# The experts' bias as one fp32r product of the 0/1 choice, with the probability multiplied in afterwards

## Chip, cores and metric

The kernel runs on one core of a Trainium2 chip. The metric is the device time of one execution in microseconds (us); the median of several runs is given.

## What is computed

The input is x, 4 images of 64 x 64 x 64, and a class token. Three layers follow: an involution over the image, a layer norm with a state space model in both directions, and a layer norm with a mixture of experts. The change lies in the last one:

```python
H = jax.nn.gelu(xf @ W1 + b1, approximate=False)          # 256 hidden values per token
probs = jax.nn.softmax(H @ Wg + bg, axis=-1)              # 8 experts
assign = jnp.argmax(probs, axis=-1)
for e in range(8):
    y = H @ Wd[e] + bd[e]
    out = out + jnp.where((assign == e)[:, None], probs[:, e:e + 1] * y, 0.0)
```

Each token takes the one expert with the highest probability, and that expert's output, its bias bd included, is multiplied by the probability. The layer's input is added to it.

## The kernel before

The kernel is a row of blocks (setup, involution, matrices, layer norm, state space, experts), each with one hand-written instruction order per engine and semaphores between the engines. At a block's end all engines wait for one another.

The function experts works on 17 items: 16 of 512 columns, each holding 1024 tokens as 8 groups (TPI) of 128 tokens, and a last small one for the 4 class tokens. A loop over windows runs on every engine; window i holds the main work of item i and preparations of items i+1 to i+4.

- TensorE (PE), in the order of its function window (L1390): hide (L1320) makes the hidden values of item i+1 in two halves; speak (L1363) makes, for one group of 128 tokens, the outputs of all 8 experts, 6 fp32r products of 128x512 each (L1374); there are 8 speaks per window, t = 0 to 7. Between them stand turn_gate (L1357, the transposition of the gate), turn_out and turn_in (transpositions for later items), judge (L1333, the logits of item i+1, after speak 4), gates (L1348), and add_bias (L1380, after speak 6).
- add_bias multiplies the transposed gate, in which each token has the probability of its expert in one of 8 places and zeros elsewhere, by bd8, which holds bd eight times along a diagonal of blocks. This is one fp32 product of 64 rows and 512 columns (L1386); it shows as two instructions in the trace. It writes the PSUM tensor pGR, which judge uses too.
- VectorE (DVE), in the order of its function window (L1594): multiply (L1505) takes the 8 experts' outputs of a group from PSUM times the gate; part (L1517) makes the low part of a piece of the hidden values of item i+1 (four pieces, between the multiplies of tiles 0 to 3); minus_sum, low and normalise prepare later items; finish (L1585) adds the bias of item i-1, read from pGR, to the experts' sum and stands behind the multiply of tile 3; choose_best (L1544) and weigh_best (L1565) make the gate of item i+1 in 11 small steps around the multiply of tile 6.
- ScalarE (ACT) does the gelu, copies the transposed gate to SBUF (keep_gate, L1442), and works on squares and copies for later items.
- GpSimd (POOL) adds the 8 experts' products of four groups in a tree (L1669, L1671, L1673, L1678), twice per window: the first tree after the multiply of tile 3, the second after that of tile 7. Between the two stands the factor of item i+3 (L1650 to L1660), with a pow at L1652, which normalise waits for.
- SP stores the results; the loads of weights, bd among them, are issued early by SP in load_rest (L475), in the block of the involution.

A speak needs one of three PSUM buffers and waits for the multiply three tiles back. judge waits for the last part of its item. finish releases pGR: judge and add_bias wait on its semaphore, finished.

Before the first item, the windows -3 to 0 only prepare (AHEAD = 4).

Of the kernel before, what the change touches and what calls it, by code (L numbers as in the profile page):

```python
# [34 lines left out]
class Tower:  # L35


    def __init__(self, nc, ctx, arrays, out):
# [19 lines left out]
        self.bd8 = sb("bd8", [2 * TILES * EX, 2 * TILES, F])  # L58
# [413 lines left out]
FFN_LOADS = 17  # L472


def load_rest(sp, g, m):  # L475
# [15 lines left out]
    for t in range(2 * TILES):  # L491
        sp.dma_start(g.bd8[EX * t:EX * t + EX, t, :], g.bd).then_inc(m.ffn_in, 16)
# [711 lines left out]
def experts(nc, g):  # L1204
# [8 lines left out]
    with ExitStack() as ctx:  # L1213
# [15 lines left out]
        pT = pLT[0:TPI * EX, 4 * TILES * EX:]  # L1229
# [16 lines left out]
        gT = sb("gT", [TPI * EX, 128])  # L1246
        gl = sb("gl", [128, 5, TPI, EX])
        gate = [sb(f"gate{n}", [128, TPI, EX]) for n in range(2)]
# [6 lines left out]
        picked = [sb(f"picked{n}", [128, TPI, F]) for n in range(2)]  # L1255
        res = [sb(f"res{n}", [128, TPI, F]) for n in range(2)]
# [8 lines left out]
        gate_turned, gate_kept, biased = sem("gate_turned"), sem("gate_kept"), sem("biased")  # L1265
# [5 lines left out]

        hflat = g.hT[:].rearrange("p b r q -> p (b r q)")
# [25 lines left out]
        with nc.Block() as block:  # L1298
            @block.tensor
            def _(pe):  # L1300
# [32 lines left out]
                def judge(i):  # L1333
# [3 lines left out]
                    if i >= 2:  # L1337
                        pe.wait_ge(finished, i - 1)
# [18 lines left out]
                def turn_gate(i):  # L1357
                    pe.wait_ge(dv, GATE * (i + 1))
                    P, G = rows(i), groups(i) * EX
                    nc.tensor.transpose(pT[0:G, 0:P], gate[i % 2][0:P, 0:groups(i), :].rearrange("p t e -> p (t e)"),  # L1360
                                        g.ident[0:P, 0:P]).then_inc(gate_turned, 1)
# [67 lines left out]
            def _(act):  # L1429
# [12 lines left out]
                def keep_gate(i):  # L1442
# [3 lines left out]
                    P, G = rows(i), groups(i) * EX  # L1446
                    nc.scalar.copy(gT[0:G, 0:P], pT[0:G, 0:P]).then_inc(gate_kept, 1)
# [39 lines left out]
                for i in range(1 - AHEAD, ITEMS):  # L1487
# [12 lines left out]
                    if there(i + 4):  # L1500
                        rest(i + 4)

            @block.vector
            def _(v):
# [39 lines left out]
                def choose_best(i):  # L1544
# [18 lines left out]
                    nc.vector.tensor_tensor(G(1), G(1), wide(s(1)), ALU.is_equal).then_inc(dv, 1)  # L1563

                def weigh_best(i):  # L1565
# [12 lines left out]
                    nc.vector.reciprocal(s(3), s(2)).then_inc(dv, 1)  # L1578
                    v.wait_ge(dv, base + 10)
                    if i >= 2:  # L1580
                        v.wait_ge(gate_turned, i - 1)
                    nc.vector.tensor_tensor(gate[i % 2][0:P, 0:T, :], G(1), s(3).unsqueeze(2).broadcast_to([P, T, EX]),
                                            ALU.mult).then_inc(dv, 1)
# [53 lines left out]
                for i in range(1 - AHEAD, ITEMS):  # L1637
                    window(i)
                finish(NCH)
# [100 lines left out]
```

## Time and profile before

| | us |
|---|---|
| runs (3) | 689.91, 690.77, 691.05 |
| median | 690.77 |
| profiled execution, its own time | 688.56 |
| its span, first to last instruction | 686.5 |

| engine | busy us | share of the span |
|---|---|---|
| PE | 608.6 | 89% |
| DVE | 495.9 | 72% |
| POOL | 403.8 | 59% |
| ACT | 263.6 | 38% |

The profile is one execution of the kernel on the chip. Times are microseconds from the span's start unless marked ns. PE is TensorE's matmuls, PEld its loads of weights, which lie beside them. L1374 is line 1374 of the kernel. out<-in names the tensor written and those read, x16 counts instructions. A matmul's end is modelled and matmuls are pipelined, so two that follow one another overlap in the rows; from the start of one group to the start of the next is the better measure. On DVE, too, an instruction can start some 0.1 us before the one ahead of it is over in the rows.

### The profile page before, as it was taken

How to read it: one execution, taken by the hardware profiler on the slowest of the kernel's cores; microseconds unless marked ns; L12 is line 12 of the kernel's file. 1: busy time of each engine (PE TensorE's matmuls, PEld its weight loads, DVE VectorE, ACT ScalarE, POOL GpSimd, SP SyncE). 2: the span in 40 equal slices, each digit the busy share in tenths (PEclk: the TensorE clock that was granted, in tenths of full speed). 3: DMA queues.
4: the chain of work that ended last, by engine and by line, in shares of the span. 5: the costliest groups of instructions: out<-in, count | busy, mean ns of one | idle time of the engine just before them, and what ended most of it. 6: DMA issues, size and time to landing. Idle time of an engine off the chain costs nothing. (4 is left out here: it accounts for less than half of the span.)

```text
span 686.5 us, 9721 instructions
## 1 busy us (share of the span) xinstructions
PE 608.6 (89%) x3015; PEld 435.9 (64%) x3015; DVE 495.9 (72%) x948; ACT 263.6 (38%) x689; POOL 403.8 (59%) x562
## 2 busy tenths in 40 slices
PE   0799899967967899999973899999999999999995
PEld 0477777754745787878752466666666666666662
DVE  6688888873895787888832567777777777777664
ACT  2132223224651222222225555555555555545310
POOL 1689999610351133333345167778777777778756
PEclk9999999997977999999985599999999999999998
DMA  6200000000000000000000000000000000000001
GB/s 249 48 1 0 0 1 1 0 0 1 0 0 1 0 1 1 0 0 0 1 0 0 1 1 16 16 17 16 17 16 16 16 16 15 3 16 17 15 17 31
DMA packets 13011, 9.75 MB, mean 14 GB/s; under 512 B 4396, under 2 KB 12716, under 8 KB 12716
## 3 DMA queue, kind: packets, MB, share of 16 engines
q1 hardware_dynamic: 12956, 9.28, 4.4%
q8 instruction: 19, 0.31, 0.2%
q14 instruction: 20, 0.16, 0.1%
q10 hardware_dynamic: 16, 0.00, 0.0%
HBM read 5.08 MB, written 4.20 MB: 14 GB/s over the span
## 5 line engine op out<-in xcount | busy, mean ns | idle before, releaser
L1374 PE MATMUL ex_pE<-ex_WdP,ex_hid 128*128 128x512 f32 x774 | 205.9, 408 | 0.0
L1374 PEld LDWEIGHTS ex_pE<-ex_WdP,ex_hid 128*128 128x128 f32 x774 | 140.0, 189 | 44.3 <-DVE ex_ms L1514 7.7
L1514 DVE TENSOR_TENSOR ex_ms<-ex_pE,ex_gate 128x512 f32<-128x512 f32 x129 | 88.9, 689 | 73.3 <-PE ex_pE L1374 71.4
L1669 POOL TENSOR_TENSOR ex_s<-ex_ms 128x1024 f32<-128x1024 f32 (+1 forms) x33 | 82.4, 2497 | 66.0 <-DVE ex_ms L1514 66.0
L723 DVE TENSOR_TENSOR inv_prod<-inv_pW,m_img 128x504 f32<-128x504 f32 x144 | 91.7, 681 | 17.4 <-PE inv_pW L638 15.7
L1195 POOL TENSOR_TENSOR hT<-hT,ssm_gelu 128x512 f32<-128x512 f32 x32 | 47.7, 1509 | 95.8 <-ACT ssm_gelu L1168 95.8
L649 PE MATMUL inv_pS<-ident,inv_prod 128*128 128x128 f32 x576 | 87.8, 275 | 6.1 <-DVE inv_prod L723 5.4
L649 PEld LDWEIGHTS inv_pS<-ident,inv_prod 128*128 128x128 f32 x576 | 70.0, 141 | 28.6 <-DVE inv_prod L723 20.7
L638 PE MATMUL inv_pW<-inv_ysb,m_conv2L 98*128 98x512 f32 x144 | 69.4, 485 | 2.3 <-DVE inv_ysb L711 2.3
L1438 ACT ACTIVATE ex_hidf<-ex_pH,b1c 128x512 f32<-128x512 f32 (+1 forms) x68 | 45.1, 664 | 60.8 <-PE ex_pH L1327 60.8
L1065 PE MATMUL ssm_y<-ssm_z,N 128*128 128x512 f32 x192 | 52.1, 408 | 6.7 <-DVE ssm_z L1130 6.5
L1151 ACT CAST ssm_z<-ssm_back 128x512 fp32r<-128x512 f32 x32 | 18.3, 618 | 102.4 <-DVE ssm_back L1127 102.4
L1520 DVE TENSOR_TENSOR ex_hid<-ex_hidf,ex_hid 128x512 fp32r<-128x512 f32 (+1 forms) x68 | 55.8, 841 | 1.2 <-ACT ex_hid L1438 1.2
L1032 PE MATMUL ssm_v<-u,LV 128*128 128x512 f32 (+1 forms) x192 | 50.1, 407 | 0.0
L1130 DVE TENSOR_TENSOR ssm_z<-ssm_back,ssm_z 128x512 fp32r<-128x512 f32 x32 | 36.1, 1169 | 19.3 <-ACT ssm_z L1151 19.3
L1671 POOL TENSOR_TENSOR ex_s<-ex_s 128x512 f32<-128x512 f32 (+1 forms) x33 | 46.5, 1409 | 2.6
L1065 PEld LDWEIGHTS ssm_y<-ssm_z,N 128*128 128x128 f32 x192 | 36.8, 194 | 17.5 <-DVE ssm_z L1130 8.9
L1438 ACT ACTIVATE ex_hid<-ex_pH,b1c 128x512 fp32r<-128x512 f32 (+1 forms) x68 | 45.2, 665 | 0.0
L1461 ACT ACTIVATE ex_sq<-ex_hs,ex_stat 128x64 f32<-128x64 f32 (+1 forms) x130 | 43.6, 351 | 0.8 <-DVE ex_stat L1528 0.8
L688 ACT COPY hT<-inv_pS 128x256 f32 (+1 forms) x32 | 10.5, 382 | 81.8 <-PE inv_pS L649 81.8
L1032 PEld LDWEIGHTS ssm_v<-u,LV 128*128 128x128 f32 x192 | 36.1, 192 | 8.1
L800 POOL TENSOR_TENSOR u<-ln_u,u 128x512 fp32r<-128x512 f32 x14 | 18.6, 1352 | 37.9 <-ACT u L869 37.9
(238 smaller groups left out, 1022.9 us busy)
## 6 DMA issues: line engine op xcount, KB each, us to landing
m_img<-in_x SPq DMA_DIRECT2D x2, 2048.0 KB, 9.2
out<-ex_res SPq DMA_DIRECT2D x16, 256.0 KB, 2.3
WdT<-in_L_ffn_Wd SPq DMA_DIRECT2D x2, 256.0 KB
W1d<-in_L_ffn_W SPq DMA_DIRECT2D x2, 64.0 KB
bd<-in_L_ffn_bd SPq DMA_DIRECT2D x8, 2.0 KB
m_Bm<-in_L_attn_fwd_B_real SPq DMA_DIRECT2D x2, 16.0 KB, 1.9
m_Bm<-in_L_attn_fwd_B_imag SPq DMA_DIRECT2D x2, 16.0 KB, 2.0
m_Bm<-in_L_attn_bwd_B_real SPq DMA_DIRECT2D x2, 16.0 KB, 2.0
```

Source lines behind the costliest of these rows:

```text
L638: nc.tensor.matmul(pW[k % NW][:], m.conv2L[:, k, :], ysb[u][:], start=True, stop=True).then_inc(weighed, 1)
L649: last = nc.tensor.matmul(pS[:, 128 * j:128 * j + 128], prod[:, k, 2 * j:2 * j + 2, :], g.ident[:], is_transpose=True, start=(k == 0 and j ...
L723: nc.vector.tensor_tensor(prod[:, k, :, lo:hi], pW[k % NW][:, :, lo:hi], rows[:, :, lo + dw:hi + dw], ALU.mult).then_inc(filtered, 1)
L1032: last = nc.tensor.matmul(out[:], g.LV[weight][:, LVI[d][t][q], :], cols(g.u[value], b, d, h, q), start=(q == 0 and (value, weight) == PAR ...
L1065: last = nc.tensor.matmul(out, g.N[weight][:, n, d, first:first + 2, :], before(zP[n][value], d, h), start=False, stop=(n == 1 and (value, ...
L1195: nc.gpsimd.tensor_tensor(t, t, act_y[n % 4][:], ALU.add).then_inc(summed, 1)
L1374: last = nc.tensor.matmul(pE[n % 3][0:P].rearrange("p e f -> p (e f)"), hid[i % 2][value][:, h, par, 128 * j:128 * j + P], WdP[weight][:, ...
L1438: last = nc.scalar.activation(o[:, h, par, 0:cols(i)], pH[par][:, 0:cols(i)], ACT.Gelu, bias=g.b1c[:, h:h + 1])
L1514: nc.vector.tensor_tensor(ms[b % NB][0:P, t % TPB, :].rearrange("p (e f) -> p e f", e=EX), pE[n % 3][0:P], gate[i % 2][0:P, t, :].unsqueez ...
L1520: nc.vector.tensor_tensor(hid[i % 2][1][:, h, par, c], hidf[:, h, par, c], hid[i % 2][0][:, h, par, c], ALU.subtract).then_inc(parted, 1)
L1669: nc.gpsimd.tensor_tensor(s4[0:P, 0:T], m[:, :, 0:4 * F], m[:, :, 4 * F:], ALU.add).then_inc(halved, 1)
L1671: nc.gpsimd.tensor_tensor(s2[0:P, 0:T], s4[0:P, 0:T, 0:2 * F], s4[0:P, 0:T, 2 * F:], ALU.add).then_inc(quartered, 1)
```

## The change

The transposed tensor is no longer the gate but the 0/1 choice, `hot`, written twice side by side (64 and 64 columns, so 128 rows after the transposition). Zeros and ones are exact in fp32r. The right side becomes `bdP`, in fp32r: its upper 64 rows hold bd rounded to fp32r, its lower 64 rows the remainder, so that one fp32r product of 128 rows gives the bias of the chosen expert. VectorE then multiplies it by the probability, kept in `best`, in a new step keep_bias, which moves it from PSUM to the SBUF tensor `bias`; finish adds `bias` and `picked`, both in SBUF. bd is loaded 16 times for 8. ScalarE and VectorE make bdP once, in the first preparing window. judge and add_bias wait for bias_kept in place of finished. turn_gate waits for step 6 of the item's 11 instead of the last.

```diff
-FFN_LOADS = 17
+FFN_LOADS = 25
...
-    for t in range(2 * TILES):
-        sp.dma_start(g.bd8[EX * t:EX * t + EX, t, :], g.bd).then_inc(m.ffn_in, 16)
+    for t in range(4 * TILES):
+        sp.dma_start(g.bd8[EX * t:EX * t + EX, t % (2 * TILES), :], g.bd).then_inc(m.ffn_in, 16)
...
                     if i >= 2:
-                        pe.wait_ge(finished, i - 1)
+                        pe.wait_ge(bias_kept, i - 1)
...
                 def turn_gate(i):
-                    pe.wait_ge(dv, GATE * (i + 1))
-                    P, G = rows(i), groups(i) * EX
-                    nc.tensor.transpose(pT[0:G, 0:P], gate[i % 2][0:P, 0:groups(i), :].rearrange("p t e -> p (t e)"),
+                    pe.wait_ge(dv, GATE * i + 6)
+                    P = rows(i)
+                    nc.tensor.transpose(pT[:, 0:P], hot[i % 2][0:P].rearrange("p v t e -> p (v t e)"),
                                         g.ident[0:P, 0:P]).then_inc(gate_turned, 1)
...
                     if i >= 1:
-                        pe.wait_ge(finished, i)
-                    P, G = rows(i), groups(i)
-                    nc.tensor.matmul(pGR[0:P, 0:F * G], gT[0:EX * G, 0:P],
-                                     g.bd8[0:EX * G, 0:G, :].rearrange("k t f -> k (t f)"),
-                                     start=True, stop=True).then_inc(biased, 1)
+                        pe.wait_ge(bias_kept, i)
+                    else:
+                        pe.wait_ge(bd_parted, 1)
+                    P = rows(i)
+                    nc.tensor.matmul(pGR[0:P], gT[:, 0:P], bdP[:], start=True, stop=True).then_inc(biased, 1)
...
-                    nc.scalar.copy(gT[0:G, 0:P], pT[0:G, 0:P]).then_inc(gate_kept, 1)
+                    P = rows(i)
+                    nc.scalar.copy(gT[:, 0:P], pT[:, 0:P]).then_inc(gate_kept, 1)
...
+                    if i == 1 - AHEAD:
+                        nc.scalar.copy(bdh[lower], bd[lower])
+                        nc.scalar.copy(bdP[upper], bd[upper]).then_inc(bd_high, 1)
...
-                    nc.vector.tensor_tensor(G(1), G(1), wide(s(1)), ALU.is_equal).then_inc(dv, 1)
+                    if i >= 2:
+                        v.wait_ge(gate_turned, i - 1)
+                    both = lambda a: a.unsqueeze(1).broadcast_to([P, 2, T, EX])
+                    nc.vector.tensor_tensor(hot[i % 2][0:P, :, 0:T, :], both(G(1)),
+                                            s(1).unsqueeze(1).unsqueeze(3).broadcast_to([P, 2, T, EX]), ALU.is_equal).then_inc(dv, 1)
...
+                def keep_bias(i):
+                    v.wait_ge(biased, i + 1)
+                    P, T = rows(i), groups(i)
+                    nc.vector.tensor_tensor(bias[i % 2][0:P, 0:T, :], pGR[0:P, 0:F * T].rearrange("p (t f) -> p t f", f=F),
+                                            best[i % 2][0:P, 0:T].unsqueeze(2).broadcast_to([P, T, F]), ALU.mult).then_inc(bias_kept, 1)
...
-                    v.wait_ge(biased, i + 1)
+                    v.wait_ge(bias_kept, i + 1)
...
-                    nc.vector.tensor_tensor(res[i % 2][0:P, 0:T, :].rearrange("p t f -> p (t f)"), pGR[0:P, 0:F * T],
-                                            picked[i % 2][0:P, 0:T, :].rearrange("p t f -> p (t f)"), ALU.add).then_inc(finished, 1)
+                    nc.vector.tensor_tensor(res[i % 2][0:P, 0:T, :], bias[i % 2][0:P, 0:T, :], picked[i % 2][0:P, 0:T, :],
+                                            ALU.add).then_inc(finished, 1)
...
                     if now:
                         multiply(i, 0)
+                    if there(i - 1):
+                        keep_bias(i - 1)
                     if more:
                         part(i + 1, 0, 0)
...
                     window(i)
+                    if i == 1 - AHEAD:
+                        v.wait_ge(bd_high, 1)
+                        nc.vector.tensor_tensor(bdP[lower], bd[lower], bdh[lower], ALU.subtract).then_inc(bd_parted, 1)
+                keep_bias(NCH)
                 finish(NCH)
```

## Rows read from the trace of the kernel before

**Rows 1.** The page's chain that ended last, shares of the span by engine and line

```profile
PE 44%; ACT 1%; POOL 1%; DVE 1%; issue 0%; POOLq 0%
PE ex_pE L1374 28%; PE ex_pGR L1343 5%; PE ex_pH L1327 5%; PE ex_pGR L1386 2%; PE ex_pXU L1308 1%; PE ex_pXU L1316 1%; PE ex_pLT L1353 1%; POOL ex_s L1669 0%; ACT ex_sq L1461 0%; ACT ex_hidf L1438 0%; ACT ex_hid L1438 0%; PE ex_pLT L1360 0%; POOL ex_s L1671 0%; POOL ex_fac L1652 0%; POOL ex_s L1673 0%
```

**Rows 2.** Chain of waits in one window: start us, us, what

```profile
590.30 0.89 PE ex_pH L1327 x6
591.19 3.00 PE ex_pE L1374 x12
...
600.11 2.02 PE ex_pGR L1343 x8
...
605.48 1.05 PE ex_pGR L1386 x2
...
608.53 0.90 PE ex_pH L1327 x5
```

**Rows 3.** Busy us in that window: PE, PEld, DVE, ACT, POOL, granted clock, DMA

```profile
590.23:608.46 18.23, 18.16 (x84) 11.95 (x83) 13.63 (x27) 9.64 (x29) 14.01 (x14) 1.00 0.05 15
```

**Rows 4.** The bias product's instructions (L1386): ns min/median/max, first and last start, forms

```profile
L1386 PE MATMUL ex_pGR<-bd,ex_gT x34: 366/589/693, 405.0 to 683.7; 64*128 64x512 f32 x32, 16*4 16x128 f32 x2
```

**Rows 5.** The gate's transposition (L1360): its loads of weights

```profile
L1360 PEld LDWEIGHTS ex_pLT<-ident,ex_gate x17: 83/111/113, 396.2 to 677.9; 128*64 128x64 f32 x16, 4*16 4x16 f32 x1
```

**Rows 6.** Timeline of DVE in that window: start us, us, line, operation

```profile
590.34 0.69 DVE L1514 TENSOR_TENSOR ex_ms<-ex_pE,ex_gate 128x512 f32<-128x512 f32 x1 [0.77 <-PE ex_pE L1374]
590.95 0.68 DVE L1541 TENSOR_TENSOR ex_xn<-ex_hs,ex_fac 128x512 f32<-128x512 f32 x1
...
593.43 1.00 DVE L1520 TENSOR_TENSOR ex_hid<-ex_hidf,ex_hid 128x512 fp32r<-128x512 f32 x1
...
598.67 0.69 DVE L1514 TENSOR_TENSOR ex_ms<-ex_pE,ex_gate 128x512 f32<-128x512 f32 x1
599.28 0.68 DVE L1591 TENSOR_TENSOR ex_res<-ex_pGR,ex_picked 128x512 f32<-128x512 f32 x1
...
604.74 0.23 DVE L1556 TENSOR_TENSOR ex_gl<-ex_gl,ex_gs 128x64 f32<-128x64 f32 x1
...
605.52 0.22 DVE L1563 TENSOR_TENSOR ex_gl<-ex_gl,ex_gs 128x64 f32<-128x64 f32 x1
...
608.57 0.69 DVE L1514 TENSOR_TENSOR ex_ms<-ex_pE,ex_gate 128x512 f32<-128x512 f32 x1 [0.78 <-PE ex_pE L1374]
```

**Rows 7.** Timeline of POOL in that window

```profile
591.11 2.78 POOL L1669 TENSOR_TENSOR ex_s<-ex_ms 128x1024 f32<-128x1024 f32 x1 [1.37 <-DVE ex_ms L1514]
...
599.44 2.40 POOL L1669 TENSOR_TENSOR ex_s<-ex_ms 128x1024 f32<-128x1024 f32 x1 [1.90 <-DVE ex_ms L1514]
...
604.11 0.73 POOL L1678 TENSOR_TENSOR ex_picked<-ex_s,ex_hs 128x256 f32<-128x256 f32 x1
...
605.20 1.65 POOL L1652 TENSOR_TENSOR ex_fac<-ex_fac,ex_half 128x8 f32<-128x8 f32 x1
...
607.77 0.20 POOL L1660 TENSOR_TENSOR ex_fac<-ex_fac 128x8 f32<-128x8 f32 x1
```

**Rows 8.** Timeline of all engines at the end of the span

```profile
673.49 0.75 POOL L1673 TENSOR_TENSOR ex_s<-ex_s 128x256 f32<-128x256 f32 x1
...
673.86 0.40 DVE L1563 TENSOR_TENSOR ex_gl<-ex_gl,ex_gs 4x16 f32<-4x16 f32 x1
...
682.64 0.71 POOL L1669 TENSOR_TENSOR ex_s<-ex_ms 4x256 f32<-4x256 f32 x1
682.71 0.69 DVE L1591 TENSOR_TENSOR ex_res<-ex_pGR,ex_picked 128x512 f32<-128x512 f32 x1 [4.02 <-POOL ex_picked L1678]
```

**Rows 9.** Timeline of SP early in the span: DMA issues

```profile
30.38 2.67 SPq L492 DMA_DIRECT2D bd<-in_L_ffn_bd  x8
```

**Rows 10.** SP's waits: waited for, us in total, times, longest us

```profile
SPq L623 <- PEq L623: 113.0, 1, 113.0
```

**Rows 11.** Timeline of ACT ahead of the first window

```profile
370.00 0.58 ACT L1453 CAST ex_u<-ex_pXU 128x512 fp32r<-128x512 f32 x1 [4.65 <-PE ex_pXU L1316]
```

**Rows 12.** The parts (L1520) of the whole span: ns min/median/max

```profile
L1520 DVE TENSOR_TENSOR ex_hid<-ex_hidf,ex_hid x68: 152/777/1187, 377.0 to 668.1; 128x512 fp32r<-128x512 f32 x64, 128x4 fp32r<-128x4 f32 x4
```

More of the change, by code:

```diff
@@ L56, in __init__ @@
         self.WdT = sb("WdT", [128, 2, EX, F])
-        self.bd8 = sb("bd8", [2 * TILES * EX, 2 * TILES, F])
+        self.bd8 = sb("bd8", [4 * TILES * EX, 2 * TILES, F])
         self.bgc = sb("bgc", [4 * EX, 1])
@@ L1228, in experts @@
         pL = pLT[:, 0:4 * TILES * EX]
-        pT = pLT[0:TPI * EX, 4 * TILES * EX:]
+        pT = pLT[:, 4 * TILES * EX:]
         W1P = [sb(f"W1P{n}", [128, HID], F32R) for n in range(2)]
@@ L1245, in experts @@
         level = sb("level", [4 * EX, CH])
-        gT = sb("gT", [TPI * EX, 128])
+        gT = sb("gT", [128, 128], F32R)
+        bdP = sb("bdP", [128, TPI * F], F32R)
+        bdh = sb("bdh", [128, TPI * F], F32R)
         gl = sb("gl", [128, 5, TPI, EX])
+        hot = [sb(f"hot{n}", [128, 2, TPI, EX]) for n in range(2)]
+        best = [sb(f"best{n}", [128, TPI]) for n in range(2)]
         gate = [sb(f"gate{n}", [128, TPI, EX]) for n in range(2)]
@@ L1255, in experts @@
         picked = [sb(f"picked{n}", [128, TPI, F]) for n in range(2)]
+        bias = [sb(f"bias{n}", [128, TPI, F]) for n in range(2)]
         res = [sb(f"res{n}", [128, TPI, F]) for n in range(2)]
@@ L1264, in experts @@
         judged, leveled, gated, tanhed, dv = sem("judged"), sem("leveled"), sem("gated"), sem("tanhed"), sem("dv")
-        gate_turned, gate_kept, biased = sem("gate_turned"), sem("gate_kept"), sem("biased")
+        gate_turned, gate_kept, biased, bias_kept, bd_parted = (sem(n) for n in ("gate_turned", "gate_kept", "biased", "bias_kept", "bd_parted"))
+        bd_high = sem("bd_high")
         spoke, chosen = sem("spoke"), sem("chosen")
@@ L1270, in experts @@
         cls_stored = sem("cls_stored")
+        bd = g.bd8[:].rearrange("k t f -> k (t f)")
+        upper, lower = slice(0, TPI * EX), slice(TPI * EX, 2 * TPI * EX)
         hflat = g.hT[:].rearrange("p b r q -> p (b r q)")
@@ L1445, in keep_gate @@
                         act.wait_ge(biased, i)
-                    P, G = rows(i), groups(i) * EX
-                    nc.scalar.copy(gT[0:G, 0:P], pT[0:G, 0:P]).then_inc(gate_kept, 1)
+                    P = rows(i)
+                    nc.scalar.copy(gT[:, 0:P], pT[:, 0:P]).then_inc(gate_kept, 1)
                 def high(i):
@@ L1577, in weigh_best @@
                     v.wait_ge(dv, base + 9)
-                    nc.vector.reciprocal(s(3), s(2)).then_inc(dv, 1)
+                    nc.vector.reciprocal(best[i % 2][0:P, 0:T], s(2)).then_inc(dv, 1)
                     v.wait_ge(dv, base + 10)
[L1580 to L1583, printed above, removed]
+                    nc.vector.tensor_tensor(gate[i % 2][0:P, 0:T, :], hot[i % 2][0:P, 0, 0:T, :],
+                                            best[i % 2][0:P, 0:T].unsqueeze(2).broadcast_to([P, T, EX]), ALU.mult).then_inc(dv, 1)
+                def keep_bias(i):
[3 more added lines that the diff above has]
+                                            best[i % 2][0:P, 0:T].unsqueeze(2).broadcast_to([P, T, F]), ALU.mult).then_inc(bias_kept, 1)
                 def finish(i):
                     v.wait_ge(reduced, NB * i + batches(i))
-                    v.wait_ge(biased, i + 1)
+                    v.wait_ge(bias_kept, i + 1)
                     if i >= 2:
```

## Prediction, made before the changed kernel ran

> **What bounds the kernel now.** I read the page first, for the engines' shares and the chain that ended last, then the chain of waits in order of time over the experts' part, then the busy time of one window, and last the timelines of VectorE (DVE) and GpSimd (POOL) inside that window. The page's chain gives TensorE (PE) 44% of the whole span and no other engine over 1%; its largest lines are the experts' matmuls, L1386, the bias, among them with 2% [rows 1]. In the experts' part the chain is an unbroken row of PE pieces that repeats every 608.53 - 590.30 = 18.23 us, one window per item [rows 2]; in one such window PE is busy 18.16 of 18.23 us at granted clock 1.00 (the 2.4 GHz level), DVE 13.63, POOL 14.01, ScalarE 9.64 [rows 3]. So PE sets the time there, and a microsecond taken from PE is gained as long as DVE and POOL keep up. The question of this change is whether they do.
>
> **What is removed and added on PE.** L1386 is one product that runs as two instructions of 64x512; 32 of its 34 records have that shape, so 16 windows have it [rows 4]. The pair takes 1.05 us of the chain [rows 2]. The new product is one fp32r instruction of 128 rows and 512 columns. Its shape and type are those of L1374, twelve of which take 3.00 us [rows 2]: 0.25 us each. That is the value I take, as the nearest row. The ends: 0.15 us (the six L1327 in 0.89 us, fp32r too but half the rows and in pairs) and 0.53 us (one of the two instructions of L1386, as if the type brought nothing). Saved per window: 1.05 - 0.25 = 0.80 us (0.52 to 0.90). Sixteen windows: 12.8 us (8.3 to 14.4). The transposition before it (L1360) loads 128 columns of weights for 64; its load takes 0.11 us now [rows 5], so twice that costs between nothing, if it lies beside a matmul as loads do, and 0.11 x 16 = 1.8 us. I take nothing.
>
> **What is added on DVE.** keep_bias reads PSUM and writes SBUF, 128x512, as finish does now: 0.68 us, next instruction 0.61 us later [rows 6]. It stands behind the first multiply of a window, and queued behind it are part(0,0), the other three parts and the multiplies of tiles 1 to 3. judge on PE waits for the last part. That part is over by 598.67, where the multiply of tile 3 starts, and judge starts at 600.11 [rows 2, 6]: 1.44 us of margin. The is_equal writes 128 elements for 64, by the rows 0.23 us for 64 and 0.68 for 512 an estimate of 0.06 us more [rows 6].
>
> **What changes without being longer.** finish now adds two SBUF tensors, where one of its inputs was in PSUM. The trace shows what that means beside POOL. normalise (L1541, two SBUF inputs) starts at 590.95, and POOL's L1669 at 591.11 takes 2.78 us, where the one at 599.44, beside the old finish, takes 2.40 [rows 6, 7]: 0.38 us lost. In turn part (L1520), two SBUF inputs of the same width as finish, takes 1.00 us at 593.43 where finish takes 0.68: 0.32 us of waiting, near the end of that L1669 at 593.89 [rows 6, 7]. The small operations suffer as well: in the tail an is_equal of 4x16 takes 0.40 us behind a POOL addition that ends at 674.24 [rows 8]. So these pairs of instructions take turns, and whoever comes second waits for most of the other. finish will come 0.16 us before L1669, so it costs POOL 0.38 us each window.
>
> The Trainium skill, "SBUF — State Buffer", section "Who interferes with whom", says that the second of such a pair is blocked for the whole of the first's run. Here the measurement differs in one place: is_equal at 605.52 keeps its 0.22 us inside the 1.65 us of POOL's pow at 605.20 [rows 6, 7]. By the rule that meeting would cost the gate up to 1.4 us a window, 0.6 more than the margin left below, and 0.2 of the 0.80 would stay, 3 us in all; the row speaks against it, and I go by the row.
>
> **The walk.** I put the new pieces into the window of rows 2, 6 and 7, every other duration kept. keep_bias moves the first part to 594.03, which swallows some of its wait for POOL; the multiply of tile 3 comes at about 599.2 instead of 598.67 (+0.54). POOL's first tree, 599.44 to 604.84 now, starts 0.54 later and loses 0.38 to finish: it ends at 605.76. choose_best's first operation with two SBUF inputs comes at 604.74 and was just clear of that tree; it and the next now wait for it, about 0.6 us together, and with the 0.06 of is_equal the gate is 0.66 us later. So the multiply of the last tile starts at about 608.5, as before, though PE now delivers that tile 0.80 us earlier, at 607.77. The factor, 604.84 to 607.97 now, ends at 608.89, before normalise asks for it (609.12). The second tree starts 0.7 us later in its window than now, so the parts wait for it longer, and the last part leaves judge about 0.8 us of the 1.44. Walked through the next windows the same way, everything on DVE comes some 0.10 us later in each (DVE and POOL need 17.53 us a round, PE 17.43). After 8 or 9 windows the margin is gone; the last 5 or 6 lose 0.1 to 0.3 us each: 1.0 us, between 0 and 3.
>
> **Costs put at nothing.** The eight more loads of bd cost SP 0.33 us each (eight take 2.67 now), 2.7 us together [rows 9], and SP then sits 113 us waiting for that block's end [rows 10]; without that cover the price were 2.7 us. ScalarE's two casts of 64x512 (0.59 us each by its cast at 370.00) fall where it waits 4.65 us for PE [rows 11], and DVE's subtraction for the low part falls between normalise and its wait for u; uncovered, together 1.9 us. The earlier wait for the choice (6 steps of 11) and judge's and add_bias's waits for bias_kept in place of finished only come earlier, and freed nobody that was late. In the tail the last full finish, at 682.71, will wait for the POOL addition that started at 682.64 and then hold up the next: 0.3 us, on the path [rows 8].
>
> **The sum.** 12.8 - 1.0 - 0.3 = 11.5 us. The profiled execution took 688.56 us, so 677.1; the median of the runs shown stands 2.2 us above it, so 690.77 - 11.5 = 679.3 us.
>
> **Rivals.** (a) DVE and POOL fall into step worse than walked: each further meeting costs 0.3 to 0.4 us (the waits in the rows), one per window beyond the margin and at most two on the path. The period is then 17.75 to 18.0, a gain of 0.25 to 0.5 us in each of some 15 windows, 4 to 7.5 us in all: 683 to 687. For it: 0.8 us of margin and four or five meetings a window. Against: in the trace every window repeats the same pattern, and most of the new lateness falls into DVE's idle time.
> (b) Slower: normalise loses its turn. It starts 0.61 us after the last multiply, L1669 0.77 after it [rows 6, 7]; a lead of 0.16 us decides. If the factor comes so late that POOL goes straight from it into L1669, normalise waits some 2.25 us. The round is then: L1669 held 0.08 + 2.25, ten DVE steps of 0.60 to 0.65 to the multiply of tile 3 (6.1), 1.15 to the held tree, 5.4 of tree with 0.2 of meetings, 3.1 of factor: 18.3 us, no gain, and one more meeting of 0.4 makes 18.7 against 18.23, 0.47 x 13 = 6 us slower: 697. By the same page's rule a wait of that length is what would happen; the longest part of the trace takes 1.19 us, half a microsecond of waiting [rows 12], which can also be because none met the long addition early. Against it: the factor ends 0.23 us ahead of normalise in the walk.
> (c) The new product costs as much as one old instruction, 0.53: 8.3 - 0.8 = 7.5 us gained, 683.3. Its type speaks against it.
> (d) The change does not do what it says on PE: the product stays two instructions, or its time reappears as a wait for the load of weights. Then nothing moves: 690.8.
>
> **How the numbers follow.** Forecast, 677 to 682.5: 0.63. (a) 0.15, (c) 0.05, (b) 0.09, (d) 0.05; still lower than 677, with the 0.15 us product, 0.03. A measurement of this kernel can tell about 0.2%, 1.4 us, from no change. Faster is the forecast, (a), (c) and the lower case, 0.86; (d) is same, 0.05; (b) is slower, 0.09. The range goes from 676.5 (14.4 us saved, nothing lost) to 687.5, the end of (a); (b) and (d) are left out.
>
> **What would show it.** Right: L1386's successor once per window at 0.25 us of chain; period near 17.45 us early and a little more late; judge with no wait, or a short one on the last part in the later windows; L1669 of the first tree at about 2.8 us; the small operations of choose_best longer than 0.23. Wrong: a period over 17.7, PE waiting for parts each window, or normalise of some 3 us.

## The result and the profile after

The changed kernel takes 681.44 us (median of 4 runs, 679.56 to 682.02) against 690.34 for the kernel before (4 runs): a ratio of 0.987, 95% interval 0.983 to 0.990. The forecast was 679.3 with a range of 676.5 to 687.5. In a later comparison of six runs on one chip the same kernel took 680.49, ratio 0.988 (0.984 to 0.992). The profiled execution took 679.56 us, span 677.8. One of the four runs with the bias inside the tree (688.96 us, further down) and a few of the kernel before fell into a slower state of the chip and are left out of every ratio.

Some words are used from here on. The period is the time from the start of one window to the start of the next. The round is the time that DVE and POOL, which wait for each other, need for their work of one window. DVE instructions with two SBUF inputs and POOL's additions take turns, and whichever comes second waits [rows 6, 7]; what they take turns at is called the port here, and the one that comes second has lost its turn.

The total came out near the forecast, but the way there is another than the one walked, and by its own signs (a period over 17.7, PE waiting for parts each window, normalise of some 3 us) the prediction was wrong about it: all three came, from the fourth window on. First the page's chain that ended last (shares of the span), to be read against [rows 1]:

```profile
POOL 14%; PE 14%; DVE 11%; issue 6%; ACT 1%; POOLq 0%; DVEq 0%
PE ex_pE L1382 9%; POOL ex_s L1694 5%; DVE ex_hid L1531 4%; DVE ex_ms L1525 4%; POOL ex_fac L1677 3%; POOL ex_s L1696 2%; PE ex_pGR L1351 2%; PE ex_pH L1335 2%; POOL ex_s L1698 1%; POOL ex_picked L1703 1%; DVE ex_bias L1601 1%; DVE ex_stat L1539 1%; PE ex_pXU L1316 0%; ACT ex_sq L1469 0%; ACT ex_hidf L1446 0%
```

PE fell from 44% to 14%: most of the experts' part now hangs on POOL and DVE. (L1382 is speak, L1525 the multiply, L1351 judge, L1335 hide, L1316 turn_in, L1396 the bias product, L1531 part, L1552 normalise, L1601 keep_bias, L1610 finish, L1694 to L1703 POOL's tree.) The busy time of an early and of a late window says when that begins; the columns are those of [rows 3]:

```profile
407.23:424.25 17.02, 17.02 (x85) 12.02 (x84) 14.08 (x28) 9.64 (x29) 13.85 (x13) 1.00 0.05 16
588.69:606.58 17.89, 17.19 (x83) 11.93 (x83) 16.09 (x30) 9.77 (x29) 14.44 (x15) 1.00 0.05 16
```

The first windows take 17.02 us with PE busy throughout, 1.21 less than before; the late ones take 17.89, in which PE idles 0.70 and DVE is busy 16.09 instead of 13.63.

**Where the 1.21 us come from.** The chain of waits after, in that early window:

```profile
407.23 0.90 PE ex_pH L1335 x6
...
416.98 1.85 PE ex_pGR L1351 x8
...
422.18 0.23 PE ex_pGR L1396
422.41 0.44 PE ex_pXU L1316 x4
```

And the chain of waits of the kernel before at its first two judges (L1343), at the two speaks ahead of the first of them and at the turn_in (L1308) behind its first bias product:

```profile
397.09 2.80 PE ex_pE L1374 x12
399.89 1.85 PE ex_pGR L1343 x8
...
406.16 0.59 PE ex_pXU L1308 x4
...
417.87 0.07 issue
417.94 2.01 PE ex_pGR L1343 x8
```

The product went from 1.05 to 0.23 (0.82 saved). The turn_in behind it went from 0.59 to 0.44 (0.15): its first load of weights now starts 0.23 ahead of its own matmul, beside the product (422.02 and 422.25), where before the change both started at 406.09. Judge went from 0.07 of "issue" and 2.01 to 1.85 (0.23): in the kernel before it had waited for finish in every window except the first, where there is no finish. Sum 1.20.

**Where they are given back.** Normalise in three windows, and POOL beside the last of them (timelines of DVE and of POOL):

```profile
408.26 0.68 DVE L1552 TENSOR_TENSOR ex_xn<-ex_hs,ex_fac 128x512 f32<-128x512 f32 x1
...
425.74 0.68 DVE L1552 TENSOR_TENSOR ex_xn<-ex_hs,ex_fac 128x512 f32<-128x512 f32 x1
...
460.63 2.87 DVE L1552 TENSOR_TENSOR ex_xn<-ex_hs,ex_fac 128x512 f32<-128x512 f32 x1 [0.37 <-POOL ex_fac L1685]
```

```profile
460.40 0.20 POOL L1685 TENSOR_TENSOR ex_fac<-ex_fac 128x8 f32<-128x8 f32 x1
460.56 2.39 POOL L1694 TENSOR_TENSOR ex_s<-ex_ms 128x1024 f32<-128x1024 f32 x1
```

Normalise comes every 17.48 us (425.74 - 408.26) where PE comes every 17.02: the round of DVE and POOL loses 0.46 us a window on PE. In the fourth window the factor ends so late that POOL goes straight into its second tree, and normalise, 0.07 us behind, waits until the addition of 2.39 is over. From there on it takes 2.87 in every window, the last part is late, and judge waits for it (timelines of DVE and PE in a late window):

```profile
592.88 1.28 DVE L1531 TENSOR_TENSOR ex_hid<-ex_hidf,ex_hid 128x512 fp32r<-128x512 f32 x2
```

```profile
594.22 2.03 PE L1351 MATMUL ex_pGR<-ex_hid,ex_WgP 128*32 128x512 f32 x8 [0.70 <-DVE ex_hid L1531]
```

### The profile page after: what moved, and what is told of

The parts are those of the page before. It is cut to its first block and busy times, and to the rows that moved or that the text cites. A ratio compares the mean times of both kernels' runs of the same rounds, so it can differ in the third digit from the quotient of the medians.

```text
span 677.8 us, 9715 instructions
## 1 busy us (share of the span) xinstructions
PE 593.3 (88%) x2998; PEld 436.9 (64%) x2998; DVE 531.1 (78%) x966; ACT 266.4 (39%) x691; POOL 410.4 (61%) x562
## 5 line engine op out<-in xcount | busy, mean ns | idle before, releaser
L1382 PE MATMUL ex_pE<-ex_WdP,ex_hid 128*128 128x512 f32 x774 | 203.7, 405 | 0.0
L1382 PEld LDWEIGHTS ex_pE<-ex_WdP,ex_hid 128*128 128x128 f32 x774 | 138.8, 187 | 41.7 <-issue 10.9
L1694 POOL TENSOR_TENSOR ex_s<-ex_ms 128x1024 f32<-128x1024 f32 (+1 forms) x33 | 84.3, 2554 | 46.8 <-DVE ex_ms L1525 46.8
L1525 DVE TENSOR_TENSOR ex_ms<-ex_pE,ex_gate 128x512 f32<-128x512 f32 x129 | 87.8, 682 | 22.9 <-PE ex_pE L1382 22.5
L1151 ACT CAST ssm_z<-ssm_back 128x512 fp32r<-128x512 f32 x32 | 18.3, 618 | 101.5 <-DVE ssm_back L1127 101.5
L1531 DVE TENSOR_TENSOR ex_hid<-ex_hidf,ex_hid 128x512 fp32r<-128x512 f32 (+1 forms) x68 | 50.2, 758 | 1.2 <-ACT ex_hid L1446 1.2
L1552 DVE TENSOR_TENSOR ex_xn<-ex_hs,ex_fac 128x512 f32<-128x512 f32 (+1 forms) x17 | 33.1, 1946 | 14.8 <-POOL ex_fac L1685 14.8
L1351 PE MATMUL ex_pGR<-ex_hid,ex_WgP 128*32 128x512 f32 (+1 forms) x136 | 34.4, 396 | 9.1 <-DVE ex_hid L1531 9.0
```

What stands on the lines that cost most here:

```text
L1351: last = nc.tensor.matmul(pGR[0:4 * EX, 0:cols(i)], WgP[:, value, par, h, :], hid[i % 2][value][:, h, par, 0:cols(i)], start=(n == 0), sto ...
L1382: last = nc.tensor.matmul(pE[n % 3][0:P].rearrange("p e f -> p (e f)"), hid[i % 2][value][:, h, par, 128 * j:128 * j + P], WdP[weight][:, ...
L1525: nc.vector.tensor_tensor(ms[b % NB][0:P, t % TPB, :].rearrange("p (e f) -> p e f", e=EX), pE[n % 3][0:P], gate[i % 2][0:P, t, :].unsqueez ...
L1531: nc.vector.tensor_tensor(hid[i % 2][1][:, h, par, c], hidf[:, h, par, c], hid[i % 2][0][:, h, par, c], ALU.subtract).then_inc(parted, 1)
L1694: nc.gpsimd.tensor_tensor(s4[0:P, 0:T], m[:, :, 0:4 * F], m[:, :, 4 * F:], ALU.add).then_inc(halved, 1)
```

## The experiments

Two theories stood against each other at first: that the lost turn makes the 17.89, or that the pieces added on DVE (keep_bias, finish with two SBUF inputs) make it by themselves. Where only the time of a window is in dispute, the period of late windows is the sharper reading, since medians of one kernel scatter over several microseconds.

**Give normalise its turn.** In the changed kernel, POOL's second tree waits for normalise:

```diff
+                        if there(i + 3):
+                            pool.wait_ge(normed, i + 4)
                     for k in range((now + 1) // 2, now):
                         tree(i, k)
```

> The changed kernel, with one more wait: GpSimd's second tree of a window starts only after normalise of that window. Theory (normalise loses its turn at the SBUF port to the tree's first addition and waits for all of it): normalise falls from 2.87 us to 0.68 in the late windows, the addition starts about 0.6 us later, and the period falls from 17.89 to the 17.5 us at which VectorE and GpSimd drifted in the first windows: 10 windows x 0.4 = 4 us, 677 to 678. Rival (VectorE is simply too full with keep_bias, whoever comes first): normalise is short, but the period stays at 17.8 to 17.9 and the time at 681 to 682.

678.05 us, ratio 0.983 (0.977 to 0.989). Timelines of DVE and POOL:

```profile
586.01 0.69 DVE L1552 TENSOR_TENSOR ex_xn<-ex_hs,ex_fac 128x512 f32<-128x512 f32 x1 [0.37 <-POOL ex_fac L1685]
```

```profile
569.15 2.40 POOL L1694 TENSOR_TENSOR ex_s<-ex_ms 128x1024 f32<-128x1024 f32 x1 [0.81 <-DVE ex_xn L1552]
...
586.78 2.40 POOL L1694 TENSOR_TENSOR ex_s<-ex_ms 128x1024 f32<-128x1024 f32 x1 [0.81 <-DVE ex_xn L1552]
```

Normalise is back at 0.69 and the period at 17.63 (586.78 - 569.15), not at the 17.5 expected. The lost turn is worth 0.26 a window. The larger part of the loss, 17.63 against 17.02, is the round itself.

**finish alone, in the kernel before.** finish moved to behind the multiply of tile 2:

```diff
                         multiply(i, 2)
+                    if there(i - 1):
+                        finish(i - 1)
                     if more:
                         part(i + 1, 1, 0)
...
-                    if there(i - 1):
-                        finish(i - 1)
```

> The kernel before, with finish moved from behind the multiply of tile 3 to behind that of tile 2, ahead of the last two parts. Theory (in the kernel before judge started 0.25 us late in every window because it waited for finish, which the page shows only as issue time): judge's loads of weights lie beside the speak ahead of them again, the period falls from 18.23 to about 17.98, and 15 windows x 0.25 make 3.8 us: 686 to 687. Rival (the gap ahead of judge has another cause, such as the change of shape of the weights): period 18.23, time 690 to 691, or slower, since the parts come later.

686.81 us, ratio 0.996 (0.993 to 0.999). The chain of waits:

```profile
445.97 0.90 PE ex_pH L1327 x5
...
463.95 0.89 PE ex_pH L1327 x6
```

A period of 17.98 against 18.23: judge's wait for finish was 0.25 a window, and it can be had without the change.

**finish without the port.** In the changed kernel, finish reads its second input from PSUM instead of picked, so the experts' sum is left out of the result:

```diff
+                    other = picked[i % 2][0:P, 0:T, :]
+                    if there(i + 3):
+                        v.wait_ge(u_high, i + 4)
+                        other = pXU[0:P, 0:F * T].rearrange("p (t f) -> p t f", f=F)
-                    nc.vector.tensor_tensor(res[i % 2][0:P, 0:T, :], bias[i % 2][0:P, 0:T, :], picked[i % 2][0:P, 0:T, :],
+                    nc.vector.tensor_tensor(res[i % 2][0:P, 0:T, :], bias[i % 2][0:P, 0:T, :], other,
```

> The changed kernel, but finish adds what lies in the PSUM tensor pXU in place of the experts' sum, in the items 0 to 13: its second input is no longer in SBUF. What it leaves out is that sum. Theory (finish, with two SBUF inputs, holds the port and delays the first tree): the first tree's first addition falls from 2.79 us to 2.40, the round of VectorE and GpSimd from about 17.5 to 17.1, normalise keeps its turn (0.68 us) or loses it only in the last windows, and the period stays at 17.05 to 17.2: 8 to 10 us less than the changed kernel, 671 to 674. Rival (the port matters little for finish, the added step on VectorE sets the period): period 17.8 to 17.9, time 680 to 682.

673.07 us, ratio 0.978 (0.973 to 0.982). Chain of waits, and the first tree on POOL's timeline:

```profile
562.06 0.90 PE ex_pH L1335 x6
...
579.18 0.90 PE ex_pH L1335 x6
```

```profile
572.35 2.40 POOL L1698 TENSOR_TENSOR ex_s<-ex_ms 128x1024 f32<-128x1024 f32 x1 [1.83 <-DVE ex_ms L1525]
```

Period 17.12, and the first tree's addition takes 2.40 where it took 2.79. With it goes all but 0.10 of what the round had over PE (17.48 against 17.02): what pushed it past PE was the meeting of finish and that addition.

**keep_bias off DVE.** In the changed kernel ScalarE multiplies the probability in, eight instructions per item, in two halves:

```diff
+                    for t in range(4 * half, min(T, 4 * half + 4)):
+                        last = nc.scalar.activation(bias[i % 2][0:P, t, :], pGR[0:P, F * t:F * t + F], ACT.Identity,
+                                                    scale=best[i % 2][0:P, t:t + 1])
...
-                    if there(i - 1):
-                        keep_bias(i - 1)
```

> The changed kernel, with keep_bias on ScalarE: eight activations of 64 columns per item, each with its probability as scale, in place of the one VectorE step. VectorE has 0.6 us less per window, ScalarE 2.8 us more. Theory (the round of VectorE and GpSimd sets the period once normalise loses its turn, and keep_bias is 0.6 us of that round): the round falls by 0.6, the first windows run at PE's 17.03 us and drift less than 0.1 us per window, normalise keeps its turn, 670 to 673. If normalise loses its turn all the same, the period is about 17.3: 674 to 676. Rival (the lost turn alone matters, and the step of 0.6 us lies in time that VectorE idles): period 17.9, 681.

679.23 us, ratio 0.987 (0.982 to 0.992), period 17.80 for 17.89: as good as nothing, so the theory missed. DVE's timeline shows why:

```profile
567.01 2.87 DVE L1572 TENSOR_TENSOR ex_xn<-ex_hs,ex_fac 128x512 f32<-128x512 f32 x1 [0.37 <-POOL ex_fac L1698]
...
570.41 1.17 DVE L1551 TENSOR_TENSOR ex_hid<-ex_hidf,ex_hid 128x512 fp32r<-128x512 f32 x1
```

Without keep_bias ahead of it, the first part comes 0.6 us sooner and spends 0.5 us waiting for POOL (1.17 against 0.68). keep_bias had filled that wait.

**The product alone, 64 rows.** In the kernel before, bd and the gate rounded to fp32r, their low parts left out; all else as it was:

```diff
-        gT = sb("gT", [TPI * EX, 128])
+        gT = sb("gT", [TPI * EX, 128], F32R)
+        bdr = sb("bdr", [TPI * EX, TPI, F], F32R)
...
-                                     g.bd8[0:EX * G, 0:G, :].rearrange("k t f -> k (t f)"),
+                                     bdr[0:EX * G, 0:G, :].rearrange("k t f -> k (t f)"),
```

> The kernel before with one part of the change alone: the bias product as one fp32r instruction of the 64 rows of the gate times bd, both rounded to fp32r; the low parts of both are left out. finish, keep_bias and the choice stay as before the change. Theory (PE alone gains 0.82 us by the product and 0.14 us by loads of weights that lie beside the matmuls again, and what the changed kernel lacks goes to keep_bias's and finish's place at the SBUF port): period 18.23 - 0.96 = 17.27, 16 x 0.96 = 15.4 us, 674 to 676; judge still waits 0.25 us for finish. Rival (VectorE and GpSimd need about 17.9 a round in any case, as late as PE lets them be): period 17.8 to 17.9 and 681.

680.71 us, ratio 0.989 (0.985 to 0.992), period 17.58: missed. The chain of waits:

```profile
575.37 0.07 issue
575.44 2.00 PE ex_pGR L1345 x8
...
580.81 0.42 PE ex_pGR L1390
581.24 0.59 PE ex_pXU L1310 x4
```

The product takes 0.42 and the turn_in behind it keeps its 0.59; the changed kernel has 0.23 and 0.44. With judge's 0.22 that is 17.02 + 0.19 + 0.15 + 0.22 = 17.58.

**Both edits together.** That kernel with finish moved to behind the multiply of tile 2, as above:

> The run above (product alone, low parts left out) with finish ahead of the last two parts. Theory (judge's wait for finish is the third part of PE's gain): period 17.02, as in the first windows of the changed kernel, another 15 x 0.25 = 3.8 us: 670 to 672. Rival (the parts, 0.6 us later, now hold judge, or the round of VectorE and GpSimd sets in): period 17.2 to 17.5, 674 to 678.

684.17 us, ratio 0.992 (0.988 to 0.996), period 17.81: a miss, slower than the product alone. Timelines of DVE and PE:

```profile
575.26 0.69 DVE L1597 TENSOR_TENSOR ex_res<-ex_pGR,ex_picked 128x512 f32<-128x512 f32 x1 [0.25 <-POOL ex_picked L1684]
```

```profile
577.21 2.04 PE L1345 MATMUL ex_pGR<-ex_hid,ex_WgP 128*32 128x512 f32 x8 [0.27 <-DVE ex_hid L1526]
```

At the shorter period the early finish has to wait for POOL's tree, and the parts queue behind it. The move that helped at 18.23 hurts here.

**The bias inside the tree.** The gate's high and low parts times bd's high part, a second product of 64 rows for bd's low part; VectorE adds h to that from PSUM (hb), POOL's last addition takes hb for h and writes the result, and there is no finish:

```diff
+                    nc.tensor.matmul(pGR[0:P], gT[:, 0:P], bdP[:], start=True, stop=False)
+                    nc.tensor.matmul(pGR[0:P], gT[upper, 0:P], bdL[:], start=False, stop=True).then_inc(biased, 1)
...
+                    nc.vector.tensor_tensor(hb[i % 2][0:P, 0:T, :], pGR[0:P, 0:F * T].rearrange("p (t f) -> p t f", f=F),
+                                            hs[i % NH][0:P, 0:T, :], ALU.add).then_inc(bias_kept, 1)
...
+                    nc.gpsimd.tensor_tensor(res[i % 2][0:P, first:first + T], s1[0:P, 0:T], hb[i % 2][0:P, first:first + T],
                                             ALU.add).then_inc(reduced, 1)
```

> Another way to the whole result: the gate's high and low fp32r parts are the 128 rows, against the high part of bd twice, and a second fp32r product of 64 rows adds the high gate times the low part of bd; VectorE makes the gate's low part from PSUM, adds the bias from PSUM to the layer's input in the place of finish, and GpSimd's last addition of the tree adds that sum, so that no finish is left and no VectorE step of 512 columns has two SBUF inputs more than before. Theory (PE's period is 17.02 plus a second product of 0.23, and the round of VectorE and GpSimd without finish at the port is at most 17.12, as with finish from PSUM): period 17.25 to 17.35, and the end is some 0.5 us shorter: 673 to 676, less than the changed kernel by 6 to 8 us. Rival (the added small step on VectorE and the wider gate push the last tile's multiply as the choice did, and normalise loses its turn): period 17.8, 680.

682.58 us (median of three runs, 676.84 to 682.63, a wide scatter), ratio 0.989 (0.980 to 0.998), period 17.66, not 17.25 to 17.35: a miss. The round is off the path, as expected, but PE is dearer. Then the same with all 128 rows in the second product:

```diff
-                    nc.tensor.matmul(pGR[0:P], gT[upper, 0:P], bdL[:], start=False, stop=True).then_inc(biased, 1)
+                    nc.tensor.matmul(pGR[0:P], gT[:, 0:P], bdL[:], start=False, stop=True).then_inc(biased, 1)
```

> The gate's bias is computed as in the run before it (high and low part of the gate times bd's high part, added to h by VectorE from PSUM, last tree addition of GpSimd writes the result), but the product with bd's low part takes all 128 rows of the gate where it took 64. Theory: what cost 0.42 us there, and kept the next load of weights from running beside a matmul, was the 64-row product; a second 128-row product costs about what the changed kernel's one does, 0.23 us. Period 17.02 + 0.23 = 17.25 (17.2 to 17.35), normalise 0.7, experts' part 15 us shorter than in the kernel before, time near 675. Rival: the second product is dear because it accumulates onto a product just made, whatever its rows; then it stays 0.4 and the period 17.6 to 17.7, time 681 to 682. Second rival: GpSimd's and VectorE's round, hidden so far under TensorE's 17.66, is itself 17.4 to 17.5, and PE is seen to wait for parts.

677.72 us, ratio 0.983 (0.979 to 0.986), period 17.38. The two products and the speak behind them, first with 64 rows in the second:

```profile
577.86 0.24 PE ex_pGR L1391
578.10 0.42 PE ex_pGR L1392
578.52 1.60 PE ex_pE L1379 x6
```

and with 128 (judge follows):

```profile
607.47 0.24 PE ex_pGR L1391
607.71 0.23 PE ex_pGR L1392
607.94 1.40 PE ex_pE L1379 x6
609.34 1.97 PE ex_pGR L1348 x8
```

The row count made the difference: 0.42 to 0.23, and 1.60 to 1.40 for the speak. Where the time goes is seen in one window of the run with 64 rows (timeline; PEld are the loads of weights):

```profile
663.10 0.19 PEld L1391 LDWEIGHTS ex_pGR<-ex_bdP,ex_gT 128*128 128x128 f32 x1
663.33 0.40 PE L1391 MATMUL ex_pGR<-ex_bdP,ex_gT 128*128 128x512 f32 x1
...
663.66 0.18 PEld L1392 LDWEIGHTS ex_pGR<-ex_bdL,ex_gT 64*128 64x128 f32 x1 [0.37 <-issue]
663.66 0.49 PE L1392 MATMUL ex_pGR<-ex_bdL,ex_gT 64*128 64x512 f32 x1
664.08 1.24 PEld L1379 LDWEIGHTS ex_pE<-ex_WdP,ex_hid 128*128 128x128 f32 x6 [0.24 <-issue]
664.08 1.67 PE L1379 MATMUL ex_pE<-ex_WdP,ex_hid 128*128 128x512 f32 x6
```

The load for the 128 rows starts 0.23 ahead of its matmul, beside the matmul before it. The load for the 64 rows, and the one for the speak behind it, start only together with their own matmuls. The period is 0.13 above the 17.25 expected, nearly all of it in a judge of 1.97 instead of 1.85, which starts just behind hb.

**The product alone, 128 rows.** The kernel before with one product of the rounded gate, written twice side by side, and bd's high over its low part; the gate's low part is left out. Then, in the same comparison, the changed kernel again.

```diff
-                    nc.vector.tensor_tensor(gate[i % 2][0:P, 0:T, :], G(1), s(3).unsqueeze(2).broadcast_to([P, T, EX]),
-                                            ALU.mult).then_inc(dv, 1)
+                    nc.vector.tensor_tensor(gate[i % 2][0:P, :, 0:T, :], G(1).unsqueeze(1).broadcast_to([P, 2, T, EX]),
+                                            s(3).unsqueeze(1).unsqueeze(3).broadcast_to([P, 2, T, EX]), ALU.mult).then_inc(dv, 1)
...
+                    nc.tensor.matmul(pGR[0:P], gT[:, 0:P], bdP[:], start=True, stop=True).then_inc(biased, 1)
```

> The kernel before with one fp32r product for the bias, as in the earlier run of the product alone, but of 128 rows: the gate is written twice side by side by VectorE, turned as 128 columns, and multiplied with bd's high part over its low part, as the changed kernel does with the choice. The gate's own low part is left out. finish stays as in the kernel before, reading PSUM. Theory: the 64-row product cost 0.43 us and exposed 0.14 us of weight loads; with 128 rows both go, and only judge's wait for finish, 0.25 us a window, stays against the changed kernel's 17.02: period 17.27 (17.2 to 17.35), time 675 to 676. Rival: the cost has nothing to do with the rows (the place behind a late gate, the type of bd): period stays 17.6, time 680 to 681. Second rival: the DVE/POOL round with a finish that reads PSUM is itself above 17.3, and PE waits for parts or for the chosen tile.

> The changed kernel itself, on the same chip and in the same rounds as the other two. Theory: as before, period 17.0 in the first three windows and 17.9 from the fourth on, ratio to the kernel before near 0.987.

677.40 us, ratio 0.981 (0.978 to 0.985), against 680.49 for the changed kernel, whose late windows again take 17.90. Chain of waits of the first of the two:

```profile
580.86 2.01 PE ex_pGR L1347 x8
...
586.22 0.24 PE ex_pGR L1392
586.46 0.44 PE ex_pXU L1312 x4
```

The row count is the cause again: 0.24 and 0.44. The period is 17.36, not 17.27: finish now holds judge up for longer (0.19 of wait on PE's timeline and a judge of 2.01).

**One product and no finish.** The bias inside the tree, with one product as in the run before; the gate's low part is left out here too:

```diff
-                    nc.tensor.matmul(pGR[0:P], gT[:, 0:P], bdP[:], start=True, stop=False)
-                    nc.tensor.matmul(pGR[0:P], gT[:, 0:P], bdL[:], start=False, stop=True).then_inc(biased, 1)
+                    nc.tensor.matmul(pGR[0:P], gT[:, 0:P], bdP[:], start=True, stop=True).then_inc(biased, 1)
```

> The run with the bias in the tree (128 rows), without its second product and without VectorE's subtraction for the gate's low part: the gate, rounded once to fp32r and written twice, times bd's high over its low part; VectorE adds h to it from PSUM, GpSimd's last tree addition writes the result, and there is no finish. Left out against the kernels before: the gate's low part. Theory: the second product was 0.23 us of the 17.38 and the longer judge (1.97 against 1.85) stays, so the period is 17.02 to 17.15, normalise 0.7, PE unbroken; experts' part 17.5 us shorter than before, time 672 to 674. Rival: VectorE's and GpSimd's round, so far hidden under 17.38, is itself 17.3 to 17.4; then PE waits for the parts or the chosen tile, and the period stays there, time 676 to 678.

677.84 us, ratio 0.980 (0.976 to 0.984), period 17.38 (578.59 - 561.21): the theory missed. PE's timeline:

```profile
578.59 2.04 PE L1347 MATMUL ex_pGR<-ex_hid,ex_WgP 128*32 128x512 f32 x8 [0.17 <-DVE ex_hb L1599]
```

Judge waits for hb, which stands behind four parts and the multiply of tile 3 in DVE's order. The rival's size was right, but PE waited for hb and not for parts or a tile. The last run puts hb where keep_bias stands in the changed kernel, puts the product behind the seventh speak again, as there, and makes POOL's last two additions one (the cuts show hb and the addition, against the run before):

```diff
+                    if there(i - 1):
+                        keep_bias(i - 1)
...
-                    if now:
-                        keep_bias(i)
...
+                def total(i):
...
+                    nc.gpsimd.tensor_tensor(res[i % 2][0:P, 0:T], s1[0:P, 0:T], hb[i % 2][0:P, 0:T], ALU.add).then_inc(reduced, 1)
```

> The run before it (one product of the rounded gate, h added from PSUM, no finish), with the order of the changed kernel: the product stands behind the window's seventh tile, and VectorE's addition of h behind the first multiply of the next window, where the parts wait for GpSimd's port anyway. GpSimd's two last additions of 128x256 become one of 128x512 behind the second tree, so the first tree is 0.8 us shorter and the factor comes sooner. Left out, as before: the gate's low part. Theory: what held the run before at 17.39 was that judge waited for the addition of h, which stood too late in VectorE's queue (0.17 us of wait and a judge of 2.03 against 1.85); with it out of the way TensorE sets the period again, 17.02 to 17.15, normalise 0.7, experts' part 17 to 19 us shorter than before, time 671 to 674. Rival: the parts now wait for the 128x512 addition behind the second tree, judge waits for the last part, and the period is 17.3 to 17.5, time 676 to 678.

671.52 us, ratio 0.974 (0.969 to 0.979). Chain of waits and busy time:

```profile
560.50 0.90 PE ex_pH L1331 x6
...
577.58 0.90 PE ex_pH L1331 x6
```

```profile
575.00:592.00 17.00, 17.00 (x84) 11.88 (x83) 14.36 (x28) 9.65 (x29) 13.75 (x14) 1.00 0.06 16
```

Period 17.08 and PE without a gap, as the theory said. It is the fastest kernel here that computes the whole layer, with the gate rounded once for the bias. The three edits of this run were not tried singly, so the share of each stays open.

## Why the prediction was right, and where it was not

**The product: right.** Valued at 0.25, it took 0.23. The rival (c) with 0.53 falls for 128 rows, though one of 64 rows came near it (0.42). So of the 0.82 saved, 0.63 came with one fp32r instruction for two of fp32 and 0.19 with the rows. The trace before already showed this price: the twelve products of two speaks take 3.00 behind hide, which has 64 rows, and 2.80, or 0.23 each, behind a transposition of 128 rows (line at 397.09). I took the 3.00.

**PE's saving: too small.** Two terms of 0.15 and 0.23 a window were missing. The sentence that failed: judge's wait for bias_kept in place of finished "only come earlier, and freed nobody that was late". The rows for it stood in the prediction's own groups: finish runs 599.28 to about 599.9 and judge starts at 600.11 [rows 2, 6]. I had measured judge's margin against the last part alone. The move of finish in the kernel before shows the 0.25 by itself. The 0.15 lies in the load of the turn_in behind the product, which I had not asked about; the runs with 64 and 128 rows show that it goes by the rows of the product. The transposition, put at nothing, takes its 0.11 on the chain before and after.

**The round: right. The loss: mis-sized.** Walked at 17.53, the round of DVE and POOL measured 17.48 in the first windows. But the loss hangs on the difference of two numbers that lie close together: 17.53 - 17.43 = 0.10 was forecast and 17.48 - 17.02 = 0.46 came. The margin was gone after three windows, not after eight or nine. Then normalise lost its turn, the mechanism of rival (b), which I had given 0.09. Its price was right in the held second tree and too high in the round: 18.3 was walked and 17.89 measured. I let finish delay the start of the first tree (1.15 us from the multiply of tile 3 to it) and counted meetings as well; measured, the tree starts 0.76 behind that multiply, and the hold shows once, in its 2.79. So (b)'s mechanism came with a gain, not a loss: 18.23 - 17.89 = 0.34 a window.

**The sum.** The starts of the bias product on PE's timelines of the two profiles say where the time was saved (us):

| bias product | before | after | saved since the row above |
|---|---|---|---|
| first | 405.04 | 405.00 | |
| fourth | 459.65 | 456.28 | 3.33 |
| fourteenth | 641.45 | 634.83 | 3.25 |
| sixteenth | 673.87 | 664.75 | 2.50 |
| end of the span | 686.5 | 677.8 | -0.4 |

Three early windows save about 1.1 each and ten late ones 0.3 each. The last two, where few preparations are left and the chain is PE's again, save 1.25 each. Less 0.4 at the end, this makes 8.7, near the 8.9 of the medians. That the forecast of 11.5 was close is luck: a saving too small (0.80 for 1.20 a window) and a loss too small (1 us for some 9) offset each other in part.

**finish and POOL: right.** The first tree's addition was forecast at 2.8 and takes 2.79 (2.40 before [rows 7]). The run with finish's input in PSUM shows that this meeting is what lifts the round over PE, but for 0.10.

**keep_bias: right in part.** It was to swallow some of the first part's wait for POOL. The run on ScalarE shows that it swallows nearly all.

**Turns at the port.** Normalise, 0.07 us behind an addition of 2.39, waited for the whole of it. The Trainium skill, "SBUF — State Buffer", section "Who interferes with whom", says that the second of such a pair is blocked for the whole of the first's run; here the trace agrees. The exception I had gone by holds as well: in the last run, too, an is_equal (0.23 from 575.96 on) runs inside POOL's pow (1.65 from 575.68 on).

**The tail: right.** The last full finish takes 1.19 us instead of 0.69, and the small addition behind it 0.79 instead of 0.45, about the 0.3 forecast:

```profile
673.52 1.19 DVE L1610 TENSOR_TENSOR ex_res<-ex_bias,ex_picked 128x512 f32<-128x512 f32 x1 [4.20 <-POOL ex_picked L1703]
```

**What was not told apart.** The costs put at nothing (eight more loads, casts ahead of the first window) were not tried by themselves. The first bias product starts at 405.00 against 405.04, so none of them shows; but in two profiles of the changed kernel that start differs by 2 us (405.00 and 403.02), about as much as either cost. The cast taken as 0.59 is 0.58 in its row [rows 11]; nothing hangs on it.

## What to carry to other kernels

When a second pair of engines runs a round only a little shorter than the bounding engine's, compute both new periods to a tenth of a microsecond before trusting the gain: whatever is saved beyond the second round is not gained, and the drift can end in a lost turn. Price a new piece from rows whose neighbours are like its own. For each wait that an edit changes, look at who starts right behind the old releaser, even where the trace lists no wait. In a queue with waits for a shared port, put added work that does not need the port into those waits, and keep late inputs of the bounding engine out from behind them.

## What was not expected of the hardware

- A 64-row fp32r product of 512 columns between products of 128 rows costs more than one of 128 rows: 0.42 against 0.23 us, and the work behind it 0.15 to 0.20 more (0.59 for 0.44, 1.60 for 1.40). The loads themselves are as long (183 and 188 ns). Filling the other 64 rows shortened the period in both pairs of runs (17.58 to 17.36 and 17.66 to 17.38). The rows above show that the load does not run beside a matmul there; why not stays open. The Trainium skill, "TensorE: Matmul & The Clock Gate", section "Step-by-step: what each phase is for", says that the row count does not matter for the time of a load; the lengths of the loads agree, the time of the whole step does not follow.
- A judge that PE reaches after a wait takes 2.01 to 2.04 us on the chain instead of 1.85, so a wait of 0.07 costs 0.23. Its load of weights then starts together with it (580.83 and 580.86 in the run of the product alone with 128 rows).
- 0.6 us of DVE work a window (keep_bias) cost next to nothing, 0.09 of the period, because it lay where a part would have waited for POOL.
